# GpSimd's tile crossings, a split layer norm, later denominators and four moved sums in a fused state-space and expert kernel

## The reference

```python
x = x + attn(layernorm(x))
x = x + ffn(layernorm(x))
# attn: 4 heads of 64, state size 128
z, xc, dt_raw, bc = split(xn @ W_in.T)
u  = silu(causal_conv4(xc) + dw_bias)
dt = clip(softplus(dt_raw + dt_bias), 1e-4, 0.1)
B, C = l2norm(bc[..., 0, :]), l2norm(bc[..., 1, :])     # each has a y half and a v half
denom = 1 + dt * kdamp + dt**2 * A
v = (v - dt * A * y + dt * u * Bv) / denom              # a scan over the 2048 steps
y = y + dt * v + dt * u * By
o = y . Cy + v . Cv
out = ((o + skip * u) * silu(z)) @ W_out.T
# ffn: softmax router over 8 experts, the best 2 of them weighted, and one shared expert
out = shared(x) + sum_e w[e] * (gelu(x @ rw1[e] + rb1[e]) @ rw2[e] + rb2[e])
```

## Time and profile before

| what | us |
|---|---|
| median of 3 runs | 554.46 (548.82, 554.51, 554.46) |
| the profiled execution | 556.07 |
| its span | 554.4 |
| mean granted TensorE clock | 0.911 of full |
| TensorE matmuls busy | 452.5 (82%) |
| VectorE busy | 461.9 (83%) |
| ScalarE busy | 256.5 (46%) |
| GpSimd busy | 287.2 (52%) |

### The profile page before, as it was taken

The page is one execution under the profiler, slowest core; times in us unless marked ns, Lnnn a source line. Parts: engine busy times, 40 slices in busy tenths (PEclk is TensorE's granted clock), DMA queues, the critical chain, the costliest instruction groups (busy, mean ns, idle before and its releaser), DMA issues.

```text
span 554.4 us, 9589 instructions
## 1 busy us (share of the span) xinstructions
PE 452.5 (82%) x3238; PEld 365.7 (66%) x3238; DVE 461.9 (83%) x1275; ACT 256.5 (46%) x501; POOL 287.2 (52%) x367
## 2 busy tenths in 40 slices
PE   5960149997989959898789968898799977998997
PEld 4840148885756648686656757687575766786886
DVE  5699986989999986889999995988999997788542
ACT  1541226564375425354565614536537542433463
POOL 2017866768108855567406756566702766777100
PEclk9985558998999977898999986989899997998999
DMA  7400000000000010000000000000000000000000
GB/s 230 142 0 0 1 1 2 1 2 1 0 1 2 0 40 0 2 1 2 1 0 2 0 21 1 1 1 1 2 1 1 1 1 21 1 2 1 2 11 9
DMA packets 8434, 7.06 MB, mean 13 GB/s; under 512 B 1593, under 2 KB 7618, under 8 KB 8258
## 3 DMA queue, kind: packets, MB, share of 16 engines
q1 hardware_dynamic: 8386, 6.46, 3.9%
HBM read 5.41 MB, written 1.05 MB: 12 GB/s over the span
## 4 chain that ended last, share of the span: by engine, by line
DVE 39%; PE 32%; POOL 15%; issue 8%; ACT 3%; DMA 0%; SPq 0%; DVEq 0%; POOLq 0%; ACTq 0%
DVE tpA L1272 5%; DVE GV L1272 5%; DVE xr L1420 5%; PE BC L590 4%; PE HB L493 4%; POOL vt L1602 4%; DVE BC L1283 3%; POOL rinv L1637 3%; PE GV L612 3%; PE HB L550 3%; POOL big L1599 3%; DVE mm L1320 2%; PE HB L600 2%; DVE GV L1283 2%; PE OO L665 2%
## 5 line engine op out<-in xcount | busy, mean ns | idle before, releaser
L590 PE MATMUL BC<-xnT,winT 128*128 128x128 f32 x512 | 83.4, 315 | 51.0 <-ACT pr L901 28.1
L590 PEld LDWEIGHTS BC<-xnT,winT 128*128 128x128 f32 x512 | 73.6, 222 | 58.1 <-issue 29.1
L1599 POOL TENSOR_TENSOR big<-mm 128x256 f32<-128x256 f32 x64 | 50.1, 783 | 83.5 <-DVE mm L1320 83.4
L1622 POOL TENSOR_SCALAR uT<-uT,skipT 128x512 f32<-128x512 f32 x8 | 15.3, 1928 | 86.9 <-DVE w L1405 53.4
L1602 POOL TENSOR_TENSOR vt<-mm 128x256 f32<-128x256 f32 x64 | 58.0, 906 | 0.0
L542 PE MATMUL HB<-xnT,w 128*128 128x512 f32 x108 | 52.0, 603 | 3.7 <-ACT gtm L986 2.1
L923 ACT ACTIVATE big<-GV 128x256 f32<-128x256 f32 x60 | 23.1, 385 | 68.1 <-PE GV L615 66.7
L612 PE MATMUL GV<-big,vt 128*128 128x128 f32 x256 | 48.2, 318 | 7.0 <-POOL vt L1602 7.0
L1318 DVE TENSOR_TENSOR mm<-BC,pr 128x512 f32<-128x512 f32 x64 | 44.2, 691 | 7.7 <-POOL vt L1602 2.4
L1611 POOL TENSOR_TENSOR mm<-ab,pr 128x256 f32<-128x256 f32 x48 | 41.3, 883 | 17.4 <-ACT pr L901 17.4
L612 PEld LDWEIGHTS GV<-big,vt 128*128 128x128 f32 x256 | 40.0, 224 | 12.9 <-POOL vt L1602 9.8
(11 more groups left out here) (215 smaller groups left out, 1165.3 us busy)
## 6 DMA issues: line engine op xcount, KB each, us to landing
xr<-in_x SPq DMA_DIRECT2D x4, 256.0 KB, 4.6
winT<-in_w_inT SPq DMA_DIRECT2D x1, 1024.0 KB, 6.0
w<-in_rw SPq DMA_DIRECT2D x1, 1024.0 KB
out<-xr SPq DMA_DIRECT2D x3, 256.0 KB, 2.3
taps<-in_dw_wT SPq DMA_DIRECT2D x1, 512.0 KB, 3.8
w<-in_sw SPq DMA_DIRECT2D x2, 128.0 KB
out<-xr SPq DMA_DIRECT2D x2, 128.0 KB, 1.8
winT<-in_w_inT SPq DMA_DIRECT2D x1, 130.0 KB, 2.6
```

The costliest lines, as they stand in the source:

```text
L590: last = pe.matmul(b[:, j * TS:(j + 1) * TS], winT[:, col:col + NS], xt, start=True, stop=True)
L1599: pool.tensor_tensor(wt[q % 8][:], m[:, 0], m[:, 3], ALU.add)
```

## The change

The constants: ScalarE's normalising operations keep step 2 (`F_XN`) but the second two of them go to step 3; the transposes go from step 3 to 4, the logarithm from 13 to 14, the scans from 15 and 16 to 16 and 17. The denominators of the four heads go from steps 10 to 13 to steps 11 to 14. `WARM` goes from (10, 1, 7) to (22, 3, 15). The crossings are queued on GpSimd ahead of the pair loop, behind a wait for the last conversion. The four sums of the last expert go behind the products of pairs 0 to 3.

```diff
-    0, 2, 3, 5, 6, 7, 8, 9, 13, 15, 17)
+    0, 2, 4, 5, 6, 7, 8, 9, 14, 16, 18)
 F_LOG_HEADS = F_BCAST + 1
-WARM = (10, 1, 7)
+WARM = (22, 3, 15)
@@ ScalarE, front_early
-                if g and k == F_XN:
-
-                    act.wait_ge(ln_rstd, ln_index(LN1, g) + 1)
-                    act.wait_ge(h_ready, USE[("xnT2", g - 2) if g >= 2 else ("xnT", g - 1)] + 1)
-                    for c in range(GT):
+                if g and F_XN <= k < F_XN + 2:
+
+                    if k == F_XN:
+                        act.wait_ge(ln_rstd, ln_index(LN1, g) + 1)
+                        act.wait_ge(h_ready, USE[("xnT2", g - 2) if g >= 2 else ("xnT", g - 1)] + 1)
+                    for c in range(2 * (k - F_XN), 2 * (k - F_XN) + 2):
                         last = act.activation(xn[:, c, :], xr[g % 3][:, c, :], ACT.Identity, bias=shift[:, c:c + 1],
                                               scale=rstd[:, c:c + 1])
-                    last.then_inc(ln_xn, 1)
+                    if k > F_XN:
+                        last.then_inc(ln_xn, 1)
@@ VectorE, front_early
-                if 1 <= k - F_BCAST < 1 + NH:
+                if 2 <= k - F_BCAST < 2 + NH:
 
-                    denominators(g, k - F_BCAST - 1)
+                    denominators(g, k - F_BCAST - 2)
@@ VectorE, after the fills
-                for slot in range(2 * DS, EXPERT_SLOT + NX * EXPERT_SLOTS):
-                    between(g, slot)
...
                     if k < KP:
                         products(KP * g + k)
+                    if 2 * DS + k < EXPERT_SLOT + NX * EXPERT_SLOTS:
+                        between(g, 2 * DS + k)
@@ GpSimd
                 W0 = 2 * PC
+                pool.wait_ge(conv, CHUNKS * (g + 1))
                 if g:
...
                 fills(g)
+                crossings(g)
                 for k in range(MID_STEPS):
...
-                    if k == 1:
-                        crossings(g)
```

## The result

The changed kernel took 536.47 us (median of 6 runs, 534.13 to 542.98) against 551.77 for the kernel before on the same chip (6 runs, 548.82 to 554.51): a ratio of 0.972, 95% interval [0.966, 0.9781], 15.3 us. The forecast of 547 and its range of 541 to 557 lie above both. Single executions of each kernel lie some microseconds apart, by where TensorE's clock halves, and the profiled one of the kernel before (556.07) is the slowest seen of it: the medians are the result, the traces show where the time lies.

The account below looks back on a forecast made before the run. VectorE and TensorE, each busy four fifths, were taken to bound the kernel through their handovers. Gains of 13.5 us at the starts less 5.3 for the scans gave -8.2, from 556.07 to 547.9, 546.3 on the median's scale: 547, range 541 to 557.

Parts of the forecast that it names:

- the scans: Group ends: scans one step later delay the last state 1.75 us in each of three groups, 5.3 us slower.
- the starts: Group starts to pair 5: earlier crossings and moved sums end TensorE's standstill, clock returns sooner; 13.5 us faster together.
- the warm-up: Kernel's front: more warm-up transposes cost nothing and bring no full clock; 0 us, bounds 0.5 slower and 3.4 faster.
- Rival 1: Group starts: clock doesn't come back sooner; starts give 7.1 us, tail takes 5.3, total 552.5 us; chance 0.23.
- Contention: Group starts: crossings beside VectorE's fills, both reading two SBUF tensors, cost 0.5 us a group, bounds 0 and 2.6.
- Rival 2: Group starts: fills and crossings exclude one another fully, 2.1 us more in each of four groups, 554.5 us; chance 0.12.
- the fourth denominators: Step 14, from moving denominators one step later: one more VectorE operation, 0.7 us, taken as absorbed.
- Rival 3: Group ends: later scans drop TensorE to half clock, 3.5 us in each of three groups, 562 us; chance 0.09.
- rival 4: Kernel's front: the warm-up works as well, bringing the full clock, 3.4 us more gained, 543.5 us; chance 0.09.
- The sums: Group starts: last expert's four sums removed before pair 0, 1.04 us; 0.26 us added behind each of pairs 0 to 3.
- Layer norm 0: Layer norm in two parts, in two steps: worth 0, bounds -0.3 and +0.5 us a group.
- The denominators' -0.1: Step 12: VectorE's wait for head 2's copy becomes one for pair 13's square, 0.1 us won.

Follow-up runs that it names:

- e10: Changed kernel with denominators and scans back in their old steps (e4's kernel again): 535.4 us, ratio to the kernel before 0.9697.
- e6: Kernel before with 44 identity transposes a group keeping TensorE busy until the first products, crossings still late: 550.2 us against 550.09.
- e7: Changed kernel with 40 identity transposes a group keeping TensorE busy in the same way as e6: 537.67 us, ratio to the kernel before 0.9757.
- e5: Kernel before with the crossings alone moved ahead of pair 0: 540.55 us against 550.09, ratio 0.9829.
- e3: Changed kernel with the short warm-up back, 10, 1 and 7 transposes: 542.13 us, ratio to the kernel before 0.9876.
- e1: Changed kernel with the crossings back in step 1, between pair 0 and pair 1 on GpSimd: 546.37 us, ratio to the kernel before 0.9945.
- e4: Changed kernel with denominators, logarithm and scans back in their old steps: 534.36 us, ratio to the kernel before 0.975.
- e12: e11 with the short warm-up, 10, 1 and 7 transposes: 537.8 us, ratio to the kernel before 0.9746.
- e11: e10 with the layer norm in one part as before: 536.01 us, ratio to the kernel before 0.9708.
- e2: Changed kernel with the last expert's four sums back ahead of pair 0: 541.11 us, ratio to the kernel before 0.9876.
- e8: e4 with the 40 identity transposes a group keeping TensorE busy: 534.03 us, ratio to the kernel before 0.9722.

## Why the forecast was wrong, step by step

Its sum was -8.2 us on the profiled execution; -20.2 was measured. By the medians 547 was 10.5 us too high: 2.7 because the kernel before has 551.77 with six runs and not 554.46 as with three, 0.7 because 547 lies above the 546.3 of that scale, and 7.1 by the sum. In the sum, by the traces, the scans are 3.9 us wrong, the starts 2.3 and the warm-up 1.8; pairs 5 to 9 cost 0.8 that it did not have. (Rival 1's 552.5 is 552.7 by its own terms.)

**The starts: mechanism right, size 2.3 short.** Forecast 3.5, 4.5, 4.5 and 1.0 us; measured 3.5, 5.4, 4.5 and 2.3, 15.8 for 13.5. Each link is in the rows above: crossings ahead of the products, no standstill, clock back 3.8 us after the restart in group 1. In group 0 it came back 4.5 us after TensorE's restart, at 79.96, and in group 2 7.4 us after it, at 325.7: more than the prediction's 7, less than the 13.0 before. Timeline of the changed kernel in the two groups, then the windows before the full clock:

```profile
75.43 2.08 PE L590 MATMUL BC<-xnT,winT 128*128 128x128 f32 x8 [6.00 <-DVE mm L1322]
...
318.33 1.59 PE L590 MATMUL BC<-xnT,winT 128*128 128x128 f32 x8 [4.33 <-DVE mm L1322]
```

```profile
79.00:80.00 1.00, 1.00 (x6) 1.00 (x6) 1.00 (x2) 0.21 (x1) 1.00 (x2) 0.52 0.00 0
325.00:326.00 1.00, 1.00 (x8) 1.00 (x7) 1.00 (x2) 0.90 (x3) 0.14 (x1) 0.64 0.00 0
```

In group 3 there was luck: in this execution the clock had fallen early and was back at 441.8, 1.2 us ahead of the restart, and pairs 0 to 5 took 11.0 us; in e10, at half clock there, they took 11.65.

Contention was taken at 0.5 a group and is 0.45: eight crossings beside the fills take 0.32 to 0.48 us instead of 0.20 to 0.30 (the last two, behind the fills, 0.25 as before), and each of the later three pairs of fills takes some 0.13 us more. The Trainium skill, page "SBUF — State Buffer", section "SBUF: two separate sides", calls the shared ports an exclusive lock, held for a whole instruction. The trace does not bear that out in full: fills that take 2.8 us alone and crossings that take 2.1 ran together in 3.2, and the price was a sixth of the 2.6 us a group that would have been the whole of the crossings laid between the fills. Rival 2 falls. Rival 1, the clock not returning sooner, falls by the clock's windows. What the prediction had not seen, e6 and e7 show in group 1: the full clock at the restart brings nothing there (12.4 us both ways) or little (1.1 us in the kernel before), since TensorE does not set the pace in that stretch.

**The scans: the step that failed.** The prediction charged 1.75 us in each of three groups, 5.3 in all; measured 0.1, 0.1 and 1.2, 1.4 in all. The failed sentence is that VectorE fills the time "until pair 14's mask (132.75; TensorE has its product ready no earlier)". The mask at 132.75 starts as the first scan ends, 129.98 plus 2.84, so that row could not say when TensorE was ready. In the changed kernel nothing covers it, and the product is seen. Timeline behind group 1's pairs, at full clock:

```profile
246.02 0.68 DVE L1164 TENSOR_TENSOR lden<-lden,ab 128x512 f32<-128x512 f32 x1
...
247.66 0.71 PE L612 MATMUL GV<-big,vt 128*128 128x128 f32 x4
247.76 0.68 DVE L1322 TENSOR_TENSOR mm<-BC,pr 128x512 f32<-128x512 f32 x1
...
249.10 0.29 DVE L1310 TENSOR_TENSOR gtm<-GV,causal 128x128 f32<-128x128 f32 x1 [0.47 <-PE GV L615]
...
249.21 0.72 POOL L1605 TENSOR_TENSOR vt<-mm 128x256 f32<-128x256 f32 x1
249.31 2.77 DVE L1153 TENSOR_TENSOR_SCAN lden<-keep,lden 128x1024 f32<-128x1024 f32 x1
...
253.22 2.28 DVE L1153 TENSOR_TENSOR_SCAN lden<-keep,lden 128x1024 f32<-128x1024 f32 x1
...
257.71 0.69 DVE L1344 TENSOR_TENSOR xi<-x 128x512 f32<-128x512 f32 x1
```

The mask starts 1.34 us behind pair 15's second product. Before it was 3.56 us, from this row to the mask of the earlier trace rows:

```profile
129.19 0.68 DVE L1320 TENSOR_TENSOR mm<-BC,pr 128x512 f32<-128x512 f32 x1
```

So VectorE idles 0.47 us, not the nearly three that the prediction had laid there. The same places of e10, with the scans in their old steps and also at full clock:

```profile
247.10 0.68 DVE L1322 TENSOR_TENSOR mm<-BC,pr 128x512 f32<-128x512 f32 x1
...
247.90 2.84 DVE L1153 TENSOR_TENSOR_SCAN lden<-keep,lden 128x1024 f32<-128x1024 f32 x1
250.66 0.26 DVE L1310 TENSOR_TENSOR gtm<-GV,causal 128x128 f32<-128x128 f32 x1
...
257.68 0.69 DVE L1344 TENSOR_TENSOR xi<-x 128x512 f32<-128x512 f32 x1
```

From pair 15's product to the last state e10 takes 10.58 us (the kernel before 10.59, at half clock) and the new order 9.95: moving the scans gained 0.6. What makes the tail even is a term the prediction called absorbed, the fourth denominators, 0.68 us at 246.02 ahead of pair 15's products. GpSimd got its 2 us back as forecast (0.72 at 249.21). And at half clock, group 2, with TensorE's product as the mask's releaser:

```profile
371.27 0.68 DVE L1322 TENSOR_TENSOR mm<-BC,pr 128x512 f32<-128x512 f32 x1
...
372.16 1.22 PE L612 MATMUL GV<-big,vt 128*128 128x128 f32 x4
...
374.24 0.29 DVE L1310 TENSOR_TENSOR gtm<-GV,causal 128x128 f32<-128x128 f32 x1 [2.08 <-PE GV L615]
...
382.36 0.69 DVE L1344 TENSOR_TENSOR xi<-x 128x512 f32<-128x512 f32 x1
```

Now 11.09 us: 2.08 idle, and the scans cost 0.5, so even the state in which the row of before was taken held a third of the price. Here the mask starts 2.97 us behind the product, so its readiness was taken only 0.6 too late. Nearly all the rest is the scans' own time: both take 2.28 us here, where it had 2.54 and 2.55, and the order of before has 2.84 and 2.54. Rival 3 needed over 2.5 a group and falls.

**Pairs 9 to 13 and group 3's tail: not in the prediction at all.** 3.6 and 1.1 us of the profiled difference, of which the later denominators give 0.1 a group (15.83 us against e10's 15.95). The rest is clock. The same projection, in both kernels after 1.45 us of idle time, ran at half clock before and at full clock after. Timeline of before, then of after:

```profile
230.74 2.02 PE L590 MATMUL BC<-xnT,winT 128*128 128x128 f32 x8 [1.45 <-DVE mm L1320]
```

```profile
220.71 1.16 PE L590 MATMUL BC<-xnT,winT 128*128 128x128 f32 x8 [1.45 <-DVE mm L1322]
```

No part of the edit goes with this: e6, with nothing of it, has 15.95 us there, e5 has 17.6, e3 with the new starts 20.6, and group 3's tail takes 14.1 to 14.2 us in ten of the twelve experiments, with crossings early or late, against 15.3 before (15.2 in e1 and e4). These 4.4 us are in the one execution profiled, at 556.07 the slowest of those seen; what sets off such a stretch stays open, and since three of the other six took 554.5 it need not be alone in having them. The prediction took only 1.6 us off for that, and by a shift, not by asking which stretches it was.

**The warm-up: rival 4 was right in part.** Forecast 0 us, bound 3.4, measured 1.8 (e12 against e11, and 42.9 less 41.1 us in the two traces). The long warm-up's own transposes, in the changed kernel, TensorE's first 17 us:

```profile
2.91 4.96 PE L487 MATMUL GV<-ident 128*128 128x128 f32 x22 [2.91 <-POOL ew L1672]
...
9.45 1.05 PE L464 MATMUL HB<-winT,xnT 128*128 128x4 f32 x8 [0.45 <-ACT xnT L815]
10.36 1.83 PE L487 MATMUL GV<-ident 128*128 128x128 f32 x15
...
14.38 3.15 PE L480 MATMUL BC<-tf,ident 16*128 16x128 f32 x16 [0.36 <-ACT tf L826]
```

And before:

```profile
9.69 1.87 PE L464 MATMUL HB<-winT,xnT 128*128 128x4 f32 x8 [0.56 <-ACT xnT L813]
```

The first 22 run at 0.23 us each, the last 15 at 0.12: by then the clock is full, and the logits take 1.05 us for 1.87. It falls again among the sixteen broadcasts, which take 3.15 us, 0.63 less than before. The prediction leaned on 7 us of unbroken half-clock work as a reason against; that work came behind gaps, and is no evidence on what 5 us of transposes do. The Trainium skill, page "TensorE: Matmul & The Clock Gate", section "Part 4: PE-mode transpose", says that transposes do not count as work for the clock. Here the measurement decides otherwise: nothing but transposes ran on TensorE before the logits' matmuls took their 1.05 us.

**Small terms.** The sums: 0.9 us at the start of each of three groups (e2), where 1.04 was taken. Layer norm 0 was right: 0.4 won and 0.6 lost in group 0. The denominators' -0.1 was right, and by the wait that was named: VectorE now waits for the square instead of the copy of head 2 (2.48 us in group 0, for 2.05):

```profile
113.94 0.43 DVE L1302 TENSOR_TENSOR BC<-BC,de 128x256 f32<-128x256 f32 x1 [2.48 <-ACT hist L919]
```

Together: starts -15.8, warm-up -1.8, pairs 5 to 9 +0.8, tails of groups 0 to 2 +1.4, denominators -0.3, and -4.4 of clock stretches in pairs 9 to 13 and group 3's tail: -20.1 by rounded stages, and -15.7 without those stretches, beside -15.3 and -18.1 by medians.

## What to carry to other kernels

Look for short work of a late-idle engine that stands between another engine's input and its use: 2.6 us on GpSimd, moved ahead of a pair loop into idle time, gave 9.5 us alone (e5). In the changed kernel's group 1 half of the gain is there by pair 1's matmuls, the time that they had waited; the other half comes by pair 5, in the stretch that TensorE used to spend at half clock behind the standstill. An operation that starts the instant another ends says nothing about when its other input was ready; before pricing its delay by that time, bound the input's readiness from the producer's own rows and at both clocks. And before any sum, compare the profiled execution with the other runs: what of its half-clock stretches the others may lack is not yours to win.

## What had not been expected of the hardware

Keeping TensorE busy for a full clock at a group's start (e6 to e8, 1.16 us for 2.07 in the first projection) bought nothing by the medians of three kernels; in one group of e6 and two each of e7 and e8 the transposes themselves held up that projection, by 1.8 to 3.0 us. In the kernel before the granted clock reads 1.00 in the windows from 8 to 11 us and in the one below, among the broadcasts, which take 0.236 us each against 0.135 later; at the very start only durations tell the clock.

```profile
16.00:17.00 1.00, 1.00 (x7) 1.00 (x7) 0.00 (x0) 0.00 (x0) 0.00 (x0) 1.00 1.07 280
```

A 4-column GpSimd operation that takes 0.20 us took 1.22 beside a scan on VectorE (254.28 in the changed kernel's group 1), and the 256-column gate 2.71, where the mean of its sixteen is 1.32.

```profile
254.28 1.22 POOL L1643 TENSOR_TENSOR du<-rinv,dtt 128x4 f32<-128x4 f32 x1
```
